# Spreading the roots of expert pairs 2 to 5 by DMA straight from SBUF instead of through DRAM

## The reference

```
x = layernorm(x + self_attention(x))          # 16 heads of 8, relative position logits
x = layernorm(x + cross_attention(x, ctx))    # causal
x = layernorm(x + moe(x))
moe: scores = sigmoid(x @ router_w.T)         # 64 experts, the best 8 of 4 groups for each token
     combine[t, e] = 2.5 * score / sum of the chosen scores   (0 where not chosen)
     routed = sum over e of combine[:, e] * (relu(x @ up[e])**2 @ down[e])
     shared = relu(x @ shared_up)**2 @ shared_down
```

## Time and profile before

| | us |
|---|---|
| median of 3 runs | 274.95 |
| lowest, highest | 274.36, 274.95 |
| profiled execution | 276.57 |
| its span | 274.8 |

### The profile page before, as it was taken

One profiled execution on the slowest core, in us unless ns is written; L12 is line 12 of the kernel. 1 busy time (PEld: TensorE's weight loads), 2 busy tenths in 40 slices (PEclk: granted clock), 3 DMA queues, 4 the chain that ended last, 5 costly groups with the idle time before them and its releaser, 6 DMA issues.

```text
span 274.8 us, 6025 instructions
## 1 busy us (share of the span) xinstructions
PE 255.9 (93%) x1929; PEld 203.7 (74%) x1929; DVE 197.8 (72%) x542; ACT 215.6 (78%) x573; POOL 149.3 (54%) x153
## 2 busy tenths in 40 slices
PE   6989999999997999999988989899998999999991
PEld 5579999688886876777665655678886888788860
DVE  2598746678888889999886953788994556855524
ACT  7562660798986988999999997688897887698861
POOL 4009000854529575110205034588998998699982
PEclk9999999999999999999999999999999999999998
DMA  5719430297976656333310003998590997498201
GB/s 126 163 29 375 150 90 0 84 215 239 298 156 183 189 173 182 96 99 105 99 47 4 1 2 92 242 239 213 170 212 23 212 232 181 144 227 198 72 0 38
DMA packets 52547, 38.47 MB, mean 140 GB/s; under 512 B 15842, under 2 KB 43172, under 8 KB 52516
## 3 DMA queue, kind: packets, MB, share of 16 engines
q1 hardware_dynamic: 52516, 38.09, 52.7%
HBM read 31.00 MB, written 7.08 MB: 139 GB/s over the span
## 4 chain that ended last, share of the span: by engine, by line
PE 71%; DVE 11%; ACT 6%; issue 5%; POOL 4%; DMA 1%; SPq 0%; DVEq 0%; ACTq 0%; POOLq 0%
PE bank L806 27%; PE bank L788 10%; PE bank L843 8%; PE bank L853 5%; PE bank L823 4%; PE bank L831 4%; ACT probs L1071 4%; POOL unit_lo L706 3%; DVE neg_max L1315 2%; PE bank L734 2%; PE bank L828 2%; DVE x_tok L1348 2%; PE bank L870 1%; PE bank L741 1%; DMA x_tok<-in_x 1%
## 5 line engine op out<-in xcount | busy, mean ns | idle before, releaser
L706 POOL TENSOR_TENSOR unit_lo<-unit,unit_hi 128x512 fp32r<-128x512 f32 x68 | 86.6, 1295 | 14.4 <-ACT unit_hi L1163 13.5
L1071 ACT ACTIVATE probs<-bank,neg_max 128x128 f32<-128x128 f32 x224 | 66.0, 429 | 1.2 <-DVE neg_max L1315 1.0
L1470 DVE SCALAR_TENSOR_TENSOR scaled<-bank,roots 128x512 f32<-128x512 f32 x64 | 43.8, 686 | 25.6 <-PE bank L806 22.8
L1162 ACT ACTIVATE unit<-scaled 128x512 f32<-128x512 f32 x68 | 42.9, 631 | 16.7 <-DVE scaled L1470 15.2
L1315 DVE TENSOR_REDUCE neg_max<-bank 128x4 f32<-128x512 f32 x56 | 38.3, 684 | 11.7 <-PE bank L831 11.3
L843 PE MATMUL bank<-ident,probs 128*128 128x128 f32 x256 | 39.4, 276 | 2.9 <-ACT probs L1071 2.8
L1163 ACT ACTIVATE unit_hi<-scaled 128x512 fp32r<-128x512 f32 x68 | 42.1, 618 | 0.0
L806 PE MATMUL bank<-unit_hi,w_parts 128*128 128x512 f32 x128 | 39.8, 392 | 0.0
L806 PE MATMUL bank<-x_hi,w_parts 128*128 128x512 f32 x128 | 39.8, 392 | 0.0
L843 PEld LDWEIGHTS bank<-ident,probs 128*128 128x128 f32 x256 | 29.5, 140 | 9.8 <-ACT probs L1071 7.3
L831 PE MATMUL bank<-k_bd,q_stk 128*128 128x512 f32 x64 | 33.9, 530 | 0.0
(11 more groups left out here) (213 smaller groups left out, 423.2 us busy)
## 6 DMA issues: line engine op xcount, KB each, us to landing
roots<-root_dram SPq DMA_DIRECT2D x62, 256.0 KB, 5.1
q_stk<-q_dram SPq DMA_DIRECT2D x16, 128.0 KB, 3.3
k_bd<-k_dram SPq DMA_DIRECT2D x32, 64.0 KB, 2.6
incoming<-in_L_ffn_up_w SPq DMA_DIRECT2D x4, 512.0 KB, 5.4
incoming<-in_L_ffn_down_w SPq DMA_DIRECT2D x4, 512.0 KB, 4.2
q_stk<-qc_dram SPq DMA_DIRECT2D x16, 128.0 KB, 2.8
k_bd<-kc_dram SPq DMA_DIRECT2D x32, 64.0 KB, 2.3
k_dram<-k_hi SPq DMA_DIRECT2D x2, 512.0 KB, 3.4
```

The lines of the kernel that those rows point to most:

```text
L706: nc.gpsimd.tensor_tensor(unit_lo[:, k % R], unit[:, k % 3], unit_hi[:, k % R], ALU.subtract).then_inc(lo_ready, 1)
L1071: last = nc.scalar.activation(probs[:, U % 3, h4 * L:(h4 + 1) * L], ps[BS[U % 3]][:, h4 * L:(h4 + 1) * L], ACT.Exp, bias=neg_max[:, U % 4, ...
L1162: nc.scalar.activation(unit[:, k % 3], scaled[:, k % 3], ACT.Square)
L1470: ins = nc.vector.scalar_tensor_tensor(scaled[:, k % 3], h, 0.0, roots[:, n % ROOT_RING, c % ROOTS], ALU.max, ALU.mult)
```

## The change

Sets 1 and 2 of the first half (pairs 2 to 5, `DIRECT` = 2 sets) are read by DMA from `root_t` in SBUF and no longer from `root_dram`. Each takes four DMAs: one for each of its 2 pairs and each half of the partitions. The source of each is one partition, read 64 times. SP issues them without waiting for `roots_kept`, which is waited for ahead of set 3. They have semaphores of their own, `roots_direct`, on which `units` waits for all four DMAs of a set. The sets from 3 on, and all of the second half, go through DRAM as before, and `loads_of` leaves out the first loads of places 1 and 2.

```diff
+DIRECT = 2
@@ loads_of
-    return n // ROOT_RING + 1 - (n % ROOT_RING < EARLY // ROOTS)
+    return n // ROOT_RING + 1 - (n % ROOT_RING < EARLY // ROOTS + DIRECT)
@@ block.sync
                 if f == 0:
                     sp.wait_ge(w_split, NB)
                     sp.wait_ge(pv_done, STAGES)
-                sp.wait_ge(roots_kept, 16 * (f + 1))
+                if f == 1:
+                    sp.wait_ge(roots_kept, 16 * 2)
                 for m in range(ROOT_SETS):
                     n = f * ROOT_SETS + m
                     if n < EARLY // ROOTS:
                         continue
                     if n >= ROOT_RING:
                         sp.wait_ge(scaled_ready, units_before(n - ROOT_RING + 1))
+                    if n < EARLY // ROOTS + DIRECT:
+                        for c in range(ROOTS):
+                            for e in range(2):
+                                row = 2 * ROOTS * m + 2 * c + e
+                                sp.dma_start(roots[e * IM:(e + 1) * IM, n % ROOT_RING, c],
+                                             root_t[row:row + 1, cols].unsqueeze(1).broadcast_to([1, IM, HT]))\
+                                    .then_inc(roots_direct[n - EARLY // ROOTS], 16)
+                        continue
+                    if n == EARLY // ROOTS + DIRECT:
+                        sp.wait_ge(roots_kept, 16)
                     some = root_dram[2 * ROOTS * m:2 * ROOTS * (m + 1), cols].rearrange("(c e) t -> e c t", e=2)
@@ units
                     if n < EARLY // ROOTS:
                         dve.wait_ge(root_copied, c + 1)
+                    elif n < EARLY // ROOTS + DIRECT:
+                        dve.wait_ge(roots_direct[n - EARLY // ROOTS], 16 * 2 * ROOTS)
                     else:
                         dve.wait_ge(roots_here[n % ROOT_RING], 32 * loads_of(n))
```

More of the change, by code:

```diff
@@ L355, in decoder_layer @@
         roots_kept = sem("roots_kept")
+        roots_direct = [sem(f"roots_direct{n}") for n in range(DIRECT)]
         roots_here = [sem(f"roots_here{n}") for n in range(ROOT_RING)]
```

## The result

| | us |
|---|---|
| before, median of 6 runs (lowest, highest) | 274.95 (274.36, 278.99) |
| after, median of 6 runs (lowest, highest) | 304.19 (300.92, 307.31) |
| ratio after / before | 1.100, 95% interval 1.094 to 1.106 |
| profiled execution after, its span | 307.31, 305.5 |

The change makes the kernel 10% slower. A ratio compares only those runs of each kernel that lie within 1.5% of its fastest, since some executions of every kernel are longer. The profiled execution is the longest of the six: most of its excess lies ahead of the change, where TensorE ran at a granted clock of 0.60 from 100 to 104 us (1.00 before). So stretches are compared from the root write to DRAM (SP's first DMA for the roots) to the end of the span. Before, that is 274.8 - 165.7 = 109.1 us; after, 305.5 - 168.3 = 137.2 us. The difference is 28.1 us.

What follows compares the result with a forecast made beforehand. It took the expert stage as bound by TensorE once running, by latency at its start. 276.57 + 28.8 (TensorE's delay) + 2.0 (clock) = 307.4, less 1.6 for the median gave 305.8, forecast 306; range 274.0 to 315 (8 in 10).

Steps and rivals of the forecast that it cites:

- The mechanism: Direct DMAs: one source partition gives only one engine's share, 26.2 GB/s; 306 us, by itself 298 to 315, chance 0.55.
- What bounds, and the gain: Expert stage bound by TensorE, its start by latency; first spread 1.3 us sooner gains 0, bounded by 0 and 0.33 us.
- SP's part: Eight issues of 0.607 us from 166.7 end at 171.6; set 3 issued 1.1 us later, still in time; cost 0.
- The transfers: Direct DMAs at 26.2 GB/s take 5.0 us each, 20.0 a set; set 1 complete at 188.0, set 2 at 208.0.
- The sign named for it: Direct DMAs: a landing time of 5 us more for each next one would show the rate by itself.
- From DVE's delay to TensorE's: Unit 6 on DVE 31.3 us late; TensorE 28.8 us late, as it was 2.5 us behind DVE's results.
- The clock: Stalls drop TensorE to 1.2 GHz and products after them run slow for a while: 2.0 us, bounds 0 and 5.
- The sum: Whole kernel: 276.57 + 28.8 + 2.0 = 307.4 us, 305.8 by the median, forecast 306.
- B: Rival on the direct DMAs: the source is no limit, 239 GB/s; time 274.9, between 274.6 and 276 us; chance 0.27.
- C: Rival on the direct DMAs: one partition gives half a share, 13.1 GB/s; 346 us; chance 0.08.
- D: Rival on the direct DMAs: milder limit, 60 to 120 GB/s; set 2 0 to 9 us late, 275 to 284; chance 0.05.
- E: Rival: the earlier start of the first spread is worth more than seen; 273.5 to 274.1 us; chance 0.05.

Runs made afterwards that it cites:

- e1: Changed kernel with each direct DMA reading 64 different source partitions once, not one 64 times: median 279.25 us, ratio 1.013; root write to end 109.1 us.
- e4: Changed kernel with the eight direct DMAs reading partitions 0, 4, ... 28 instead of 4 to 11: 287.45 us, ratio 1.044.
- e6: Changed kernel with its eight direct DMAs issued in turn from set 1 and set 2 (partitions 4, 8, 5, 9, 6, 10, 7, 11): 291.70 us, ratio 1.056.

## Why the prediction was right, and where its steps were off

The forecast was 306 us and the median 304.19. The mechanism held; that the number came so close is partly luck, as two errors in the sum went opposite ways.

- **What bounds, and the gain.** Right: the wait removed was worth 0. e1 shows it, with the transfers fast and the start 1.3 us earlier: 109.1 us before and with it.
- **SP's part.** Half right. Unhindered, the eight issues take 0.6 us each (e1) and set 3 is in time. I had them leave at 0.6 us in the changed kernel too, where they take 4.77. It should have made no difference, as the queue was never short of work: the last direct DMA, issued at 190.3, landed at 206.8, and with earlier issues its bytes would have stood behind the same transfers. No run tests that.
- **The transfers.** The mechanism was right and the size nearly: 26.2 GB/s was chosen as one engine's share, without a row of one source partition, and 27.5 measured. The sign named for it came as well: the first three DMAs take 4.2 us more each to land, with issues 0.6 us apart, and so land 4.8 us apart. From the fifth on that time no longer grows, as SP is held. Set 1 was complete 21.0 us after its first issue (190.35 - 169.37), forecast 22.3. Set 2 followed after 16.6 us, forecast 20.0. Of those 3.4 us the rate gives 0.9; the rest is a term I had left out, that set 2 is read at another outlet (partitions 8 to 11) than set 1 (4 to 7) and overlaps its end:

```profile
188.00:190.00 2.00, 0.00 (x0) 0.00 (x0) 0.00 (x0) 0.00 (x0) 0.00 (x0) 0.50 0.89 66
```

  In these 2 us the engines move some 77 kB more than at 27.5 GB/s, which is worth about 2.8 us (an estimate from this row). e4 and e6 show the same overlap.
- **From DVE's delay to TensorE's.** Counted from the root write, unit 6 starts 38.59 us after it, against 11.96 before: 26.6 us late, forecast 31.3. I then took off 2.5 us for TensorE's lag. That step failed. TensorE was not waiting at `expert_up(10)`. (The wait of `expert_up(k)` is for a count of k - 3, that is for units up to k - 4: `expert_up(8)` needs unit 4, `expert_up(10)` unit 6.) It was held earlier, at the transposition of `x_tok`, which stands behind unit 6 in DVE's order. TensorE after, then the same two instructions before:

```profile
181.00 0.39 PE L819 MATMUL bank<-unit_lo,w_parts 128*128 128x512 f32 x1
191.10 1.22 PE L819 MATMUL bank<-x_hi,w_parts 128*128 128x512 f32 x2 [9.71 <-DVE scaled L1485]
192.12 0.63 PE L819 MATMUL bank<-x_lo,w_parts 128*128 128x512 f32 x1
208.13 0.47 PE L903 MATMUL bank<-ident,x_tok 128*128 128x128 f32 x1 [15.39 <-DVE x_tok L1361]
208.26 1.20 PE L819 MATMUL bank<-unit_hi,w_parts 128*128 128x512 f32 x2
...
213.72 0.63 PE L819 MATMUL bank<-unit_hi,w_parts 128*128 128x512 f32 x2
```
```profile
179.29 0.28 PE L890 MATMUL bank<-ident,x_tok 128*128 128x128 f32 x1
179.33 0.71 PE L806 MATMUL bank<-unit_hi,w_parts 128*128 128x512 f32 x2
```

  `expert_down(4)`, right behind that transposition, was still to be done: it starts 39.9 us after the root write (208.26 - 168.34), against 13.6 before (179.33 - 165.70). So TensorE came back 26.3 us late where DVE was 26.6 late: the lag was worth 0.3 us and not 2.5.
- **The clock.** Forecast 2.0 us. TensorE's last product before the first stall ended at 181.4; the granted clock fell between there and 188, was 0.50 in the row of 188 to 190 above, 0.51 from 208 to 213.5 and 1.00 from 213.5 to 219. Full clock is 2.4 GHz, half of it the lower level of 1.2. `expert_down(4)` to `expert_down(6)` took 213.72 - 208.26 = 5.5 us, before 183.07 - 179.33 = 3.7, with a wait of 0.38 us for `x_t` in it: 1.7 us net, worked out from rows and not isolated by a run. With 26.3 it makes 28.0, and the stretch measured is 28.1.
- **The sum.** 30.8 us forecast over the kernel before, 29.2 by the medians, 28.1 by the stretch. Two errors partly cancel: 4.7 us too much for DVE's delay, and 2.2 too little behind it. The clock was 0.3 too much.
- **The rivals.** B (the source is no limit) is refuted by the 27 GB/s; C (half a share) and D (60 GB/s and more) by the same number; E by e1. The 120 GB/s below which the transfers were to cost time isn't tested closely: 58 GB/s cost 10.5 us (e4), 205 nothing (e1), and nothing between was run. D's price for 60 GB/s, 9 us, is near e4's.

## What to carry to other kernels

Before a DMA broadcasts from SBUF, count the groups of four partitions that its source spans (with the four 32 further as the same group): one of them gave 26 to 27 GB/s here with 2, 4 or 16 engines, and four, eight or sixteen groups 25 to 27 each. One row spread over 64 partitions took 4.8 us for 131 kB. The detour through DRAM, 2.3 us once and then an estimated 0.55 us a row at 239 GB/s, was cheaper for the eight rows here. And look first whether the wait that is to be saved has anything behind it: here 0.33 us of waiting was followed by 0.89 us of idle time on another chain, so there was nothing to win.

## What the runs showed of the hardware that I had not expected

- Slow transfers are seen on the issuing engine: an issue that takes 0.6 us took 4.77, the time of one DMA's transfer. With fast transfers the same instruction took 0.6 again (e1), so here the long issues are no cost of the issue itself.
- The order of the issues alone was worth 12.8 us (e6), as two outlets then work at once (55 GB/s instead of 27).
- The engines' share tells little of the bytes moved: 0.89 at 27 GB/s, 0.90 at 102, 1.02 at 398.
